# Layer 1, keys and values: the rows of all 25 tiles of nodes are summed, measured and normed ahead of the products

## The chip, the core and the metric

The program runs on one core of a Trainium2 chip. The metric is the device time of one launch in microseconds (us), as the median of three runs. Five engines work side by side and wait for each other through semaphores: TensorE (PE in the profile; PEld is its weight load), VectorE (DVE), ScalarE (ACT), GpSimd (POOL) and SyncE (SP, which only issues DMAs). DMAs are also issued from the queues of ScalarE and GpSimd.

## The reference, cut to what matters

Two layers of a graph network on 3125 nodes with 256 features (25 tiles of 128 nodes). Layer 0 ends with a mixture of experts with the two best experts of each node. Layer 1 begins with the sum of the experts' outputs, a layer norm, and from the normed rows both a sum over the graph's edges and a linear attention:

```python
x = x + _L0_ffn_ref(_layernorm(x)[None], ...)[0]      # gates[:, 0] * y0 + gates[:, 1] * y1
xn = _layernorm(x, axis=-1)
x = x + _L1_gnn_ref(xn, src, dst, edge_weight, ...) + _L1_mix_ref(xn[None], ...)[0]
# in _L1_gnn_ref
neighbor_emb = segment_sum(edge_val[:, None] * xn[edge_src], edge_dst)
# in _L1_mix_ref, _phi(x) = where(x > 0, x + 1, exp(x))
k_phi, v = _phi(xn @ Wk + bk), xn @ Wv + bv
kv, k_sum = einsum('blhd,blhe->bhde', k_phi, v), k_phi.sum(axis=1)
```

## The kernel before, in words

`build` runs the stages one after another, each a block at whose end all engines meet. The stage of this text is `keys_and_values`; ahead of it stands `gated_experts`, behind it `attend` (queries, attention and the output product) and `feed_forward`.

**What comes in.** The experts left two rows for each node in memory. They are loaded in five groups of five tiles (GT = 5), each group in two halves (s = 0 and 1, one for each of a node's two experts) of 640 KB, into three buffers `got`. Group g of g >= 3 takes the buffer of group g - 3 and waits for `taken` (line 1559).

**Rows.** For each tile VectorE adds the two halves with their gates into X (`add`, line 1601), measures the row (`measure`, line 1607, bn_stats), and for a part of several tiles works out the variance (`spreads`, lines 1615 to 1621). ScalarE takes the root (`roots`, line 1704), VectorE finishes 1/std and the shift (`scales`, lines 1628, 126 to 129 and 1630), and ScalarE writes the normed rows XN (`norm`, line 1708). SyncE stores each group of XN to `table` (line 1569). Before the change the three parts are tiles 0 to 4, 5 to 15 and 16 to 24. The first ten tiles are summed ahead of the products; the other fifteen are summed three at a time within steps 0 to 4, and tiles 5 to 24 are normed within steps 2 to 6.

**Steps.** There are 25 steps, one for each tile: TensorE turns the normed tile (line 1750), ScalarE copies it out (`keep`, line 1699), TensorE makes keys and values (line 1760), VectorE adds the bias (lines 1639, 1640) and cuts the negative part (line 1644), ScalarE takes its exponential (line 1734), VectorE puts the key together (line 1656), and TensorE adds it into the sum of key times value (line 1768).

**The head of the edges.** The nodes with most edges are treated by `Head`, one job a step for 24 steps. VectorE marks (`mark`, lines 825 and 836), ScalarE weighs with nine activations a job (`weigh`, line 846), TensorE multiplies (line 860) and every second step VectorE adds the result (line 884). ScalarE does jobs 0 and 1 directly behind `keep(0)`, and job i + 2 in step i. VectorE makes ready for them with eight short operations (`split_weights`, lines 784 to 787) and the marks of the first two jobs and of the first two groups of edges (lines 689, 697); before the change this stands ahead of the first sum.

**The other edges.** GpSimd waits until all five groups of `table` are stored and then gathers messages (`gather`, lines 654 and 656), six to a group of edges, for groups 0 to 5 at most: four groups of buffers, then one more group for each that TensorE has used (line 715). Groups 0 to 3 are used in steps 16, 19, 22 and 24. From group 6 on the gathers belong to the next block.

The order is written out by hand; each engine works off its own queue in the order of the code. On ScalarE, and this is what the change moves:

```python
roots(0); act.wait_ge(shift_ready, 1); norm(*parts[0])
load(act, 3, 1); load(act, 4, 1)
act.wait_ge(head.split, 8); keep(0)
for j in range(2): head.weigh(act, j)
for i in range(NT):
    if i + 1 < NT: keep(i + 1)
    if i in norming: norm(*norming[i])
    # exp of step i; weigh(i + 2); move of the edge groups beside step i
    if i in scaling: roots(scaling[i])
```

Of the kernel before, what the change touches and what calls it, by code (L numbers as in the profile page):

```python
# [19 lines left out]
NT = -(-N // P)  # L20
# [35 lines left out]
GT = 5  # L56
NG = NT // GT
# [1468 lines left out]
def keys_and_values(nc, const, routing, rows, cleared, X, XN, XNT, table, kv, kw, kv_bias, heads, more, edge_sums, groups, counts, digits, low, joint, room, counted):  # L1526
# [4 lines left out]
    parts = ((0, GT), (GT, 16), (16, NT))  # L1531
    adding = {i: range(2 * GT + 3 * i, 2 * GT + 3 * i + 3) for i in range(5)}
    scaling = {1: 1, 4: 2}
    norming = {2: (5, 9), 3: (9, 13), 4: (13, 16), 5: (16, 21), 6: (21, NT)}
    with ExitStack() as ctx:
# [30 lines left out]
        def _(sp):  # L1566
# [6 lines left out]
            for g in range(4):  # L1573
                load(sp, g, 0)
            store(0)
            load(sp, 4, 0)
            for g in range(1, NG):
                store(g)
# [13 lines left out]
        def _(dve):  # L1592
            c = Chain(dve, chain)
# [38 lines left out]
            def step(i):  # L1632
                k = i % 2
                more_rows = adding.get(i, ())
# [6 lines left out]
                for t in more_rows:  # L1641
                    add(t, 0)
                c.settle()
                ts(neg[k][:, :], key[k][:, :], 0.0, None, ALU.min).then_inc(cut, 1)
                for t in more_rows:
                    add(t, 1)
                if more_rows:
                    c.settle()
                for t in more_rows:
                    measure(t)  # L1650
# [10 lines left out]
                if i in scaling:  # L1661
                    spreads(scaling[i])
                    scales(scaling[i])
# [4 lines left out]
            head.split_weights(dve)  # L1668
            for j in range(2):
                head.mark(dve, j)  # L1670
            for e in range(2):
                edge_sums.mark(dve, e)
            for g in range(2):
                for i in range(g * GT, (g + 1) * GT):
                    add(i, 0)
                if g:
                    scales(0)
                c.settle()
                for i in range(g * GT, (g + 1) * GT):
                    add(i, 1)  # L1680
                c.settle()
                for i in range(g * GT, (g + 1) * GT):
                    measure(i)
                if g == 0:
                    spreads(0)
# [10 lines left out]
        def _(act):  # L1696
# [24 lines left out]
            load(act, 3, 1)  # L1721
            load(act, 4, 1)
# [4 lines left out]
            for i in range(NT):  # L1727
                if i + 1 < NT:
                    keep(i + 1)
                if i in norming:  # L1730
                    act.wait_ge(shift_ready, 2 if i < 5 else 3)
                    norm(*norming[i])
# [6 lines left out]
                if i in scaling:  # L1739
                    roots(scaling[i])  # L1740
# [1662 lines left out]
```

## Time and profile before

| | us |
|---|---|
| median of three runs (2177.54 to 2179.3) | 2177.92 |
| the profiled execution's own time | 2177.88 |
| its span (first to last instruction) | 2175.8 |
| TensorE busy in the span (83%) | 1802.7 |
| VectorE busy (57%) | 1249.2 |
| ScalarE busy (33%) | 708.5 |
| GpSimd busy (45%) | 984.2 |
| the stage `keys_and_values`, from 1134 to 1290 of the span | 156 |

Times in a row of the trace count from the start of the span. A row of the timeline has the start, how long the merged instructions took together, engine, line, operation, what is written and read, the count, and in brackets how long the engine had been idle and for whom. Instructions that overlap on one engine begin before the one ahead has ended, so that ten of 0.48 us take 4.16. The shares are means over stages with different limits; what this change is worth has to be read from its own stage.

### The profile page before, as it was taken

What the parts mean: (1) busy time and instruction counts of PE and PEld (TensorE: products, weight loads), DVE (VectorE), ACT (ScalarE), POOL (GpSimd) and SP (SyncE); (2) the same over time, 40 slices, a digit from 0 to 9 for tenths busy, and PEclk for the clock granted to TensorE, in tenths of its full rate; (3) what the DMA queues carried; (4) which work ended last, traced back from release to release, by engine and by line L of the source; (5) the groups of instructions that cost most, each with busy time, mean ns of one, the idle gap of its engine ahead of it and who ended that gap; (6) DMA issues with size and microseconds to landing.
All of it is one profiled execution on the core that took longest, in us unless ns stands there. A gap on an engine that the chain in (4) does not pass through costs nothing. (4 is left out here: it accounts for less than half of the span.)

```text
span 2175.8 us, 35585 instructions
## 1 busy us (share of the span) xinstructions
PE 1802.7 (83%) x10583; PEld 1413.6 (65%) x10584; DVE 1249.2 (57%) x3264; ACT 708.5 (33%) x1624; POOL 984.2 (45%) x1571
## 2 busy tenths in 40 slices
PE   7499689876485999999975999869999764999976
PEld 5266466554354999999962556546776642888865
DVE  6654796985565454444458657734454575333336
ACT  4222334443530121212127941123322231233324
POOL 0576786785111222222220547878877000455542
PEclk9999899988696999999986899979999886999998
DMA  7565554554641101011114324444444227122234
GB/s 237 153 155 139 151 143 122 148 139 109 252 182 46 37 29 37 30 36 33 33 48 138 97 61 158 114 124 112 137 123 122 86 90 320 56 65 63 65 80 133
DMA packets 171241, 239.50 MB, mean 110 GB/s; under 512 B 74145, under 2 KB 139261, under 8 KB 168692
## 3 DMA queue, kind: packets, MB, share of 16 engines
q0 software_dynamic: 42336, 112.74, 18.4%
q1 hardware_dynamic: 116884, 113.45, 16.1%
q10 hardware_dynamic: 11904, 11.96, 1.7%
q8 instruction: 47, 0.77, 0.1%
q14 instruction: 70, 0.57, 0.1%
HBM read 184.86 MB, written 56.12 MB: 111 GB/s over the span
## 5 line engine op out<-in xcount | busy, mean ns | idle before, releaser
L656 POOL DMA_INDIRECT agg_message<-table,edges_src x638 | 624.4, 979 | 177.7 <-POOL agg_rest L654 172.2
L2825 PEld LDWEIGHTS ex_p_h<-ex_xT,ex_own_up 128*128 128x128 f32 (+1 forms) x2464 | 281.3, 192 | 2.7 <-issue 1.4
L2825 PE MATMUL ex_p_h<-ex_xT,ex_own_up 128*128 128x128 f32 (+1 forms) x2464 | 282.0, 276 | 1.0 <-DVE ex_xT L2876 1.0
L2784 POOL DMA_INDIRECT ex_x<-moe_in,route_token_at x58 | 57.3, 987 | 311.8 <-PE ex_p_x L2815 242.3
L2880 DVE COPY ex_own_up<-moe_up 128x1280 f32 x114 | 100.5, 882 | 168.7 <-PE ex_p_h L2825 167.9
L654 POOL MEMSET agg_rest<- 128x1 f32 x638 | 75.6, 119 | 185.0 <-DMA table<-layer_XN 74.9
L715 PE MATMUL agg_partial<-agg_message,moe_up 128*64 128x321 f32 x638 | 113.7, 495 | 44.2 <-issue 22.0
L2950 POOL DMA_INDIRECT ex_x<-moe_in,route_token_at x66 | 64.3, 975 | 174.1 <-PE ex_p_x L2981 93.8
L2868 ACT ACTIVATE ex_gate_h<-ex_p_h 128x640 f32<-128x640 f32 x56 | 39.4, 704 | 315.3 <-PE ex_p_h L2825 315.3
L3021 ACT COPY ex_own_up<-moe_up 128x1024 f32 x66 | 68.9, 1046 | 209.9 <-PE ex_p_h L2994 169.4
L2994 PEld LDWEIGHTS ex_p_h<-ex_xT,ex_own_up 128*128 128x128 f32 x1024 | 119.3, 195 | 16.2 <-issue 14.9
L2994 PE MATMUL ex_p_h<-ex_xT,ex_own_up 128*128 128x128 f32 x1024 | 124.3, 281 | 4.7 <-issue 1.1
L3045 DVE TENSOR_SCALAR ex_hT<-ex_p_h,ex_up_b 128x128 f32<-128x128 f32 x256 | 72.1, 344 | 90.8 <-PE ex_p_h L2994 90.8
L3003 PE MATMUL ex_p_y<-moe_down,ex_hT 128*128 x512 | 115.8, 379 | 0.0
L727 ACT COPY agg_span<-agg_partial 128x321 f32<-128x321 f32 (+1 forms) x108 | 43.0, 398 | 216.4 <-PE agg_partial L719 201.2
L715 PEld LDWEIGHTS agg_partial<-agg_message,moe_up 128*64 128x64 f32 x638 | 47.6, 151 | 87.8 <-issue 60.0
L3003 PEld LDWEIGHTS ex_p_y<-moe_down,ex_hT 128*128 128x128 f32 x512 | 94.8, 190 | 11.5
L715 PE MATMUL agg_partial<-agg_message,agg_onehot 128*64 128x256 f32 x638 | 86.3, 407 | 19.1 <-PEq L111 8.7
L2793 POOL DMA_INDIRECT moe_out<-ex_y,route_row_at x56 | 56.6, 1012 | 81.8 <-DVE ex_y L2885 77.6
L2174 PE MATMUL ff_p_h<-ff_xT,layer_w 128*128 128x320 f32 x320 | 92.1, 441 | 0.5 <-ACT ff_xT L2105 0.5
L2189 PE MATMUL ff_p_y<-layer_w,ff_hT 128*128 128x256 f32 x400 | 90.2, 379 | 0.9 <-ACT ff_hT L2123 0.9
L719 PE MATMUL agg_partial<-agg_span,agg_shift 128*128 128x321 f32 (+2 forms) x212 | 85.6, 487 | 0.0
(666 smaller groups left out, 3708.3 us busy)
## 6 DMA issues: line engine op xcount, KB each, us to landing
moe_up<-in_f_w SPq DMA_DIRECT2D x8, 1386.0 KB, 20.1
agg_message<-in_edge_rows SPq DMA_DIRECT2D x54, 192.0 KB, 3.9
agg_message<-table,edges_src POOLq DMA_INDIRECT x638
sums<-agg_span SPq DMA_DIRECT2D x107, 80.2 KB
moe_up<-in_f_w SPq DMA_DIRECT2D x4, 2048.0 KB, 14.7
moe_down<-in_f_w SPq DMA_DIRECT2D x4, 2048.0 KB, 31.5
sums<-agg_span SPq DMA_DIRECT2D x107, 64.0 KB
moe0b_down<-in_f_w SPq DMA_DIRECT2D x8, 768.0 KB, 9.3
```

The costliest lines, as they stand in the source:

```text
L654: pool.memset(self.rest[:, :], 0.0).then_inc(self.paused, 1)
L656: pool.indirect_dma_start(out=to[:, k * w:k * w + D], out_offset=None, in_=self.table, in_offset=bass.IndirectOffsetOnAxis(ap=self.edges.s ...
L715: mm = pe.matmul(self.partial[h * W:(h + 1) * W, 0:w], hot[:, k * W:(k + 1) * W], msg[:, k * w:(k + 1) * w], start=(k % RUN == 0), stop=(g ...
L719: mm = pe.matmul(self.partial[to, 0:w], self.slot_shift(g)[:, to], self.held(g - 1), start=False, stop=True)
L2174: mm = pe.matmul(p_h[q % 2][:, s * 512:s * 512 + GH], w1_[:, c * FF + q * P:c * FF + (q + 1) * P], xT[:, c * GN + s * GH:c * GN + (s + 1) ...
L2189: mm = pe.matmul(p_y[n % 2][:, 0:D], hT[:, q * GN + n * P:q * GN + (n + 1) * P], w2_[:, q * D:(q + 1) * D], start=(q == 0), stop=(q == M - 1))
L2825: return pe.matmul(to, own_up[:, o:o + n], xT[:, k * D + c * P:k * D + (c + 1) * P], start=(c == 0), stop=(c == 1))
L2880: dve.tensor_copy(own_up[:, a:b], at(up, e * U0 + a, b - a)).then_inc(up_copied, 1)
L2994: mm = pe.matmul(p_h[k][:, q * P:(q + 1) * P], own_up[k][:, c * H1 + q * P:c * H1 + (q + 1) * P], xT[:, k * D + c * P:k * D + (c + 1) * P] ...
L3003: mm = pe.matmul(p_y[k][:, 0:D], hT[k][:, q * P:(q + 1) * P], at(down, ex[k] * (HQ * D) + q * D, D), start=(q == 0), stop=(q == HQ - 1))
L3021: act.copy(own_up[k][:, :], at(up, expert(act, r, k) * (2 * H1), 2 * H1)).then_inc(up_copied, 1)
L3045: ins = dve.tensor_scalar(hT[k][:, q * P:(q + 1) * P], p_h[k][:, q * P:(q + 1) * P], at(up_b, ex[k] * HQ + q, 1), 0.0, ALU.add, ALU.max)
```

## The change

All 25 tiles are summed and measured on VectorE ahead of step 0. The parts become tiles 0 to 4, 5 to 19 and 20 to 24; ScalarE takes the three roots and norms all 25 tiles before `keep(0)`. `split_weights` and the first marks move from ahead of the sums to behind them. SyncE issues the loads of groups 3 and 4 itself, both halves, in place of one half each on ScalarE, and all stores behind all loads.

```diff
-    parts = ((0, GT), (GT, 16), (16, NT))
-    adding = {i: range(2 * GT + 3 * i, 2 * GT + 3 * i + 3) for i in range(5)}
-    scaling = {1: 1, 4: 2}
-    norming = {2: (5, 9), 3: (9, 13), 4: (13, 16), 5: (16, 21), 6: (21, NT)}
+    parts = ((0, GT), (GT, 4 * GT), (4 * GT, NT))
+    measured = {0: 0, 3: 1, 4: 2}
...
-            for g in range(4):
+            for g in range(3):
                 load(sp, g, 0)
-            store(0)
-            load(sp, 4, 0)
-            for g in range(1, NG):
+            for g in range(3, NG):
+                for s in range(2):
+                    load(sp, g, s)
+            for g in range(NG):
                 store(g)
...
             def step(i):
...
-                for t in more_rows:
-                    add(t, 0)
...
-                for t in more_rows:
-                    add(t, 1)
-                if more_rows:
-                    c.settle()
-                for t in more_rows:
-                    measure(t)
...
-                if i in scaling:
-                    spreads(scaling[i])
-                    scales(scaling[i])
...
-            head.split_weights(dve)
-            for j in range(2):
-                head.mark(dve, j)
-            for e in range(2):
-                edge_sums.mark(dve, e)
-            for g in range(2):
+            for g in range(NG):
                 for i in range(g * GT, (g + 1) * GT):
                     add(i, 0)
-                if g:
-                    scales(0)
+                if g in (1, 4):
+                    scales(g // 4)
                 c.settle()
                 for i in range(g * GT, (g + 1) * GT):
                     add(i, 1)
                 c.settle()
                 for i in range(g * GT, (g + 1) * GT):
                     measure(i)
-                if g == 0:
-                    spreads(0)
+                if g in measured:
+                    spreads(measured[g])
+            scales(2)
+            head.split_weights(dve)
+            for j in range(2):
+                head.mark(dve, j)
+            for e in range(2):
+                edge_sums.mark(dve, e)
...
             norm(*parts[0])
-            load(act, 3, 1)
-            load(act, 4, 1)
+            for n in (1, 2):
+                roots(n)
+                act.wait_ge(shift_ready, n + 1)
+                norm(*parts[n])
             act.wait_ge(head.split, 8)
             keep(0)
...
-                if i in norming:
-                    act.wait_ge(shift_ready, 2 if i < 5 else 3)
-                    norm(*norming[i])
...
-                if i in scaling:
-                    roots(scaling[i])
```

What it does to the engines' queues, at the two places that the prediction speaks of. ScalarE, from the first root of the stage on, before (L1704 are roots, L1708 norms, L1699 `keep`, L846 `weigh`, L1734 the exponential):

```order
L1704 ACT_TABLE_LOAD
L1704 ACTIVATE kv_root<-kv_var 128x5
L1708 ACTIVATE layer_XN<-main_X,kv_shift,kv_rstd 128x256 x5
L1562 DMA kv_got<-moe_out 128x5x256 x2
L1699 COPY layer_XNT<-kv_p_x 128x2x128
L846 ACTIVATE layer_gw<-head_low,layer_gw 128x128 x9
L846 ACTIVATE head_pieces<-head_low,layer_gw 128x128 x9
L1699 COPY layer_XNT<-kv_p_x 128x2x128
L1734 ACT_TABLE_LOAD
```

The same place with the change, where these lines are L1692, L1696, L1687 and L1721:

```order
L1692 ACT_TABLE_LOAD
L1692 ACTIVATE kv_root<-kv_var 128x5
L1696 ACTIVATE layer_XN<-main_X,kv_shift,kv_rstd 128x256 x5
L1692 ACTIVATE kv_root<-kv_var 128x15
L1696 ACTIVATE layer_XN<-main_X,kv_shift,kv_rstd 128x256 x15
L1692 ACTIVATE kv_root<-kv_var 128x5
L1696 ACTIVATE layer_XN<-main_X,kv_shift,kv_rstd 128x256 x5
L1687 COPY layer_XNT<-kv_p_x 128x2x128
L846 ACTIVATE layer_gw<-head_low,layer_gw 128x128 x9
```

Twenty norms and two roots now stand ahead of `keep(0)`. With them go four table loads: before, each of the two later roots stood between exponentials and brought one for itself and one for the exponential behind it.

VectorE in step 0, from the bias on, before (L1601 are sums, L1607 measures):

```order
L1639 TENSOR_TENSOR kv_v<-kv_p_kv,kv_kb 128x2x128
L1640 TENSOR_TENSOR kv_key<-kv_p_kv,kv_kb 128x256
L1601 SCALAR_TENSOR_TENSOR main_X<-kv_got,main_gates,main_X 128x256 x3
L1644 TENSOR_SCALAR kv_neg<-kv_key 128x256
L1601 SCALAR_TENSOR_TENSOR main_X<-kv_got,main_gates,main_X 128x256 x3
L1607 BN_STATS kv_stats<-main_X 128x6 x3
L825 TENSOR_TENSOR head_low<-layer_w,edges_low 128x768
```

And with the change, from the two first jobs' marks on into step 0:

```order
L825 TENSOR_TENSOR head_low<-layer_w,edges_low 128x768
L836 TENSOR_SCALAR head_joint<-layer_w,edges_joint 128x100 x6
L689 TENSOR_SCALAR agg_onehot<-edges_node,edges_rel,edges_weight 128x64 x12
L697 TENSOR_SCALAR agg_shift<-edges_apart,edges_step 128x128
L1637 TENSOR_TENSOR kv_v<-kv_p_kv,kv_kb 128x2x128
L1638 TENSOR_TENSOR kv_key<-kv_p_kv,kv_kb 128x256
L1640 TENSOR_SCALAR kv_neg<-kv_key 128x256
L825 TENSOR_TENSOR head_low<-layer_w,edges_low 128x768
```

The sums and measures are gone from the steps; the first marks stand directly ahead of step 0, behind all sums.

## Rows read from the trace of the kernel before

**Rows 1.** Busy time by stretches of the stage; then clock, DMA share, GB/s

```profile
1134.00:1156.00 22.00, 1.24 (x4) 0.57 (x4) 20.00 (x70) 6.45 (x8) 3.02 (x2) 0.50 0.77 249
1156.00:1221.00 65.00, 46.79 (x187) 26.87 (x188) 45.03 (x154) 59.58 (x149) 6.43 (x12) 0.74 0.31 99
1221.00:1290.00 69.00, 66.35 (x332) 37.71 (x331) 45.47 (x147) 52.49 (x150) 33.20 (x62) 1.00 0.24 69
```

**Rows 2.** Timeline of ScalarE: keep(0), (1), (2), (10), (15)

```profile
1156.42 0.37 ACT L1699 COPY layer_XNT<-kv_p_x 128x256 f32<-128x256 f32 x1
...
1163.10 0.35 ACT L1699 COPY layer_XNT<-kv_p_x 128x256 f32<-128x256 f32 x1
...
1165.79 3.32 ACT L846 ACTIVATE layer_gw<-head_low,layer_gw 128x128 bf16<-128x128 bf16 x9 [0.61 <-DVE head_low L825]
1169.02 0.35 ACT L1699 COPY layer_XNT<-kv_p_x 128x256 f32<-128x256 f32 x1
...
1220.21 0.34 ACT L1699 COPY layer_XNT<-kv_p_x 128x256 f32<-128x256 f32 x1
...
1239.23 0.34 ACT L1699 COPY layer_XNT<-kv_p_x 128x256 f32<-128x256 f32 x1
```

**Rows 3.** Issues of ScalarE's first load of got, and its landing

```profile
L1562 ACTq DMA_DIRECT2D kv_got<-moe_out x1: 438/438/438, 1135.0 to 1135.0; - x1
DMA to landing us min/median/max: 6.9/6.9/6.9
```

**Rows 4.** Timeline of VectorE ahead of the steps

```profile
1136.05 1.50 DVE L786 CAST layer_gw<-edges_weight 128x72 bf16<-128x72 f32 x1
...
1138.35 0.20 DVE L786 CAST layer_gw<-layer_gw 128x72 bf16<-128x72 f32 x1
...
1139.55 0.56 DVE L825 TENSOR_TENSOR head_low<-layer_w,edges_low 128x768 bf16<-128x768 bf16 x1
...
1143.83 4.16 DVE L1601 SCALAR_TENSOR_TENSOR main_X<-kv_got,main_gates,main_X 128x256 f32<-128x256 f32 x10
...
1149.80 0.17 DVE L1615 TENSOR_TENSOR kv_mean<-kv_stats 128x5 f32<-128x5 f32 x1
...
1150.70 2.06 DVE L1601 SCALAR_TENSOR_TENSOR main_X<-kv_got,main_gates,main_X 128x256 f32<-128x256 f32 x5
1152.68 0.18 DVE L1628 RECIPROCAL kv_rstd<-kv_root 128x5 f32<-128x5 f32 x1
...
1153.70 0.17 DVE L1630 SCALAR_TENSOR_TENSOR kv_shift<-kv_mean,kv_rstd 128x5 f32<-128x5 f32 x1
...
1155.88 1.73 DVE L1607 BATCH_NORM_STATS2 kv_stats<-main_X 128x6 f32<-128x256 f32 x5
```

**Rows 5.** Timeline of ScalarE: a root and five norms

```profile
1197.80 0.21 ACT L1704 ACTIVATE kv_root<-kv_var 128x9 f32<-128x9 f32 x1
...
1199.32 2.57 ACT L1708 ACTIVATE layer_XN<-main_X,kv_shift,kv_rstd 128x256 f32<-128x256 f32 x5 [1.05 <-DVE kv_shift L1630]
```

**Rows 6.** Timeline of TensorE: steps 2 and 3

```profile
1169.42 3.78 PE L1760 MATMUL kv_p_kv<-layer_kw,layer_XNT 128*128 128x512 f32 x4 [1.84 <-ACT layer_XNT L1699]
1173.00 1.33 PE L860 MATMUL head_sum<-head_joint,layer_gw 128*128 128x150 bf16 x9
1174.12 1.16 PE L1768 MATMUL kv_p_a<-kv_v,kv_key 128*128 128x129 f32 x4
1175.07 0.63 PE L1750 MATMUL kv_p_x<-const_ident,layer_XN 128*128 128x128 f32 x2
1175.49 1.95 PE L1760 MATMUL kv_p_kv<-layer_kw,layer_XNT 128*128 128x512 f32 x4
```

**Rows 7.** Timeline of GpSimd: its first work, its first gather, the next block's first

```profile
1134.97 2.53 POOL L766 IOTA layer_w<- 128x768 bf16 x1 [3.24 <-POOLq L111]
...
1212.93 0.10 POOL L654 MEMSET agg_rest<- 128x1 f32 x1 [74.94 <-DMA table<-layer_XN]
...
1289.45 0.10 POOL L654 MEMSET agg_rest<- 128x1 f32 x1 [18.45 <-POOLq L111]
```

More of the change, by code:

```diff
@@ L1633, in step @@
                 k = i % 2
-                more_rows = adding.get(i, ())
                 dve.wait_ge(kv_made, i + 1)
```

## The prediction

> **What bounds the stage now.** The page's shares say nothing about one stage, so I cut the stage into stretches first [rows 1]. From 1134 to 1156 VectorE is the busy engine (20.0 of 22 us) and TensorE does next to nothing. From 1156 to 1221 it is ScalarE, 59.6 of 65 us; TensorE has 46.8 us and a granted clock of 0.74. From 1221 to 1290 TensorE has 66.4 of 69 us at full clock. So ScalarE sets the pace of the steps in the middle, and the question is what the change takes from it there and what it puts ahead of it.
>
> The timeline of ScalarE gives the pace [rows 2]. The start of `keep` (L1699) marks a step. From keep(10) at 1220.21 to keep(15) at 1239.23 there are five steps of 3.80 us: one copy, one exponential, nine weighings. From keep(0) at 1156.42 to keep(10) it takes 63.8 us, far more than ten times 3.80, because sums on VectorE, norms, roots and table loads on ScalarE and a half-clocked TensorE stand in those steps. That is what the change could win. The price is in front: keep(0) comes later. From keep(10) on both kernels do the same work in the same order, so the shift of keep(10) is the answer, if nothing behind it takes it up. I work out both halves.
>
> **First half: when keep(0) comes.** In the changed kernel VectorE has nothing ahead of the sums but three fills, so it waits for group 0. Its later half is issued at 1135.0 and lands 6.9 us after, at 1141.9 [rows 3]. The first sum starts then, not at 1143.83 [rows 4]: 1.9 us are won, though 7.8 us of work have been taken from in front of it, because that work was hiding the load.
>
> From there, with the distances in [rows 4]: a group of five tiles takes 1149.80 - 1143.83 = 5.97 us; `spreads` 1150.70 - 1149.80 = 0.90; group 1 with `scales(0)` in its midst runs from 1150.70 to the end of its measures at 1157.61, so 6.91. Groups 2 and 3 are two more of 5.97, then `spreads(1)` at 0.90. Group 4's first five sums and `scales(1)` are 1150.70 to 1153.87, so 3.17. Sum: 5.97 + 0.90 + 6.91 + 5.97 + 5.97 + 0.90 + 3.17 = 29.8, and the shift of part 1 is there at 1171.7.
>
> Do the loads keep up? The first stretch moved 249 GB/s on average with a DMA share of 0.77 [rows 1], so at a full share 249 / 0.77, about 320 GB/s (an estimate from this row). A group is 1.31 MB, 4.1 us, against 5.97 us of VectorE. Groups 3 and 4 are asked for when groups 0 and 1 are used and needed two groups later. I cost the loads at nothing; if one is late, its own 4.1 us is the price.
>
> ScalarE now norms 15 tiles: 3 x 2.57 = 7.7 us [rows 5], to 1179.4, and only behind them in its queue comes the root of part 2 (0.21), though VectorE has had the variance ready since 1171.7 + 2.06 + 1.73 + 0.90 = 1176.4. VectorE thus idles some 3.4 us. `scales(2)` takes 1153.87 - 1152.68 = 1.19 [rows 4], to 1181.1; the last five norms take 2.57, to **1183.7**.
>
> Behind `scales(2)` VectorE does `split_weights`, for which `keep(0)` waits too. Before, it took from 1136.05 to 1139.55, 3.50 us, but 1.30 of that is the first CAST (1.50, against 0.20 for the same cast later) while GpSimd filled its first iota from 1134.97 to 1137.50 [rows 4, 7]. GpSimd is long done with that at 1181, so I take 2.2 us and 1183.3, which leaves the norms as the last to come. The Trainium skill ("SBUF — State Buffer", section "SBUF: two separate sides") says that VectorE and GpSimd share a port pair under an exclusive lock; by that rule the long cast was a wait for the lock and won't recur. If it recurs after all, keep(0) is at 1184.6, 0.9 us later: this goes into the range. The marks (1139.55 to 1143.83, 4.28 us) end at 1187.6, before the first keys and values are made (below, keep(0) + 0.4 + 3.78 = 1187.9), so they lie beside TensorE.
>
> keep(0) comes at 1183.7, against 1156.42: **27.3 us later**.
>
> **Second half: from keep(0) to keep(10).** keep(1) comes after two jobs of weighing, 1163.10 - 1156.42 = 6.7 us, as before [rows 2]. keep(2): 1169.02 - 1163.10 = 5.9 less the 0.6 for which `weigh` waited for VectorE's mark behind the sums [rows 2], so 5.3 us (the table load for the exponential stays in it). Then eight steps of 3.80 = 30.4. Together 42.4 us, if TensorE keeps up.
>
> It doesn't quite. Step 2's products run at half clock now: 3.78 us for keys and values against 1.95 in step 3 [rows 6]. ScalarE's two jobs of weighing and the table load still leave TensorE with little before step 2, and I expect that again. At half clock TensorE needs 3.78 + 1.33 + 1.16 + 0.63 = 6.9 us for step 2 [rows 6]; started 0.35 us behind keep(2), at keep(0) + 12.35, it is through at + 19.3, step 3's product (1.95, full clock) at + 21.2, and VectorE's bias and cut (1.1 us) let ScalarE go on at + 22.3. On ScalarE's own pace that exponential stood at + 19.9. So 2.4 us are lost once; from then on TensorE has less than 3.80 us of work a step. Total 42.4 + 2.4 = **44.8 us, 19.0 less than the 63.8 before**. Which half clock stretches stay is the weak point. The Trainium skill ("TensorE: Matmul & The Clock Gate", section "HAM oscillation") says that bursts with waits between them let the clock fall again; by that rule the short bursts of steps 0 to 2 are throttled here too, and the dense steps behind are not.
>
> **Behind keep(10): nothing.** The table is complete earlier: the last norm ends at 1183.7 instead of about 1209, so gathers start some 25 us sooner than 1212.93. They end in four groups of buffers and wait for TensorE's step 16. In the third stretch TensorE is busy 66.4 of 69 us and so waits for no message [rows 1]; GpSimd instead stood 18.45 us at the end until the next block began [rows 7]. Early gathers have no taker. SyncE's stores and the four small loads behind them also move forward, with no one waiting. Four table loads of ScalarE are gone; they are part of the 19.0, not added to it.
>
> **Sum.** + 27.3 - 19.0 = + 8.3 us. 2177.88 + 8.3 = 2186.2. The profiled execution is at the median of the runs (2177.92), so the forecast for the median is **2186.2 us**. Sums between the products were nearly free only where another engine was last; still, 15 tiles ahead cost 27 us with the norms and the idle root, and took 19 from the steps.
>
> **Rivals.**
> 1. *TensorE has its full clock from step 2 on.* For it: the steps are denser. Against: steps 0 to 2 contain the same waits for ScalarE. The 2.4 us go: + 5.9, 2183.8.
> 2. *Half clock lasts longer.* If two further steps run at half clock, each takes 7.1 us of TensorE (6.9 and a little for wider jobs) instead of 3.80 of ScalarE: + 3.3 each, so + 14.9, 2192.8. For it: the second stretch had a mean clock of 0.74 [rows 1], so that half clock (0.50) held for about half of it. Against: it lay behind waits for sums and norms that are gone.
> 3. *The stored table is what the end waits for* (the other side). If groups 0 to 5 or what follows them hung on the gathers, the stage's end would come forward with them. It decides if any product of edges waits for its messages. All 25 us would turn + 8.3 into - 17, so 2161; a third of it would just cancel the loss. Against: the 18.45 us that GpSimd stood idle, and a TensorE without gaps in the last stretch [rows 1, 7]. This needs the trace to hide a wait.
> 4. *The loads are late.* One group late by its own 4.1 us: + 12.4, 2190.3. Against: the estimate of 4.1 against 5.97 us.
>
> Even if every step ran at ScalarE's 3.80 from keep(0) on, keep(0) to keep(10) would be 38.0 us, and the change still + 1.5 us. That is the lower end of what the steps can give, and it excludes a gain by this path.
>
> **How the numbers follow.** Forecast 0.60; rival 1 0.14; rival 2 0.08; rival 4 0.07; rival 3 0.05; and 0.06 that something unpriced (steps at the lower end, or a later stage that takes up the shift) brings it to between 0 and + 4. A measurement of this kernel tells 0.2%, 4.4 us, from no change. Slower by more than that: forecast and rivals 1, 2 and 4, less 0.03 for rival 1 with a keep(0) that is 1.5 us early: 0.86. Within: 0.06 + 0.03 = 0.09. Faster: 0.05. The forecast's own terms: keep(0) by - 1 (marks and loads better) to + 1 (the long cast), the clock by - 2.4 to + 3.3 (one step more at half clock). The range reaches down past rival 1 to + 3.1 and up to rival 4: 2181 to 2191.
>
> **What the profile would show.** Right: VectorE's first sum at about 1142; a gap of 3 to 4 us on VectorE before the last `scales`; keep(0) at 1184 (1 us either way); keep(10) at 1228.5; keep-to-keep 3.80 us from step 4 on; one table load for the exponential in the stage; first gather near 1187, with a GpSimd idle ahead of step 16 and again at the block's end; the next block's start some 8 us later than 1289.5, and everything behind it shifted by the same. Wrong: sums that wait for a landing between groups (rival 4), a half clock in steps 4 to 6 (rival 2), TensorE waiting for messages in the kernel before and not now (rival 3), or the next block's start shifted by 8 us but the end of the program not.

## The result, and the profile after

| | before | after |
|---|---|---|
| median of eight runs, same chip (us) | 2178.09 | 2186.11 |
| ratio, 95% interval | | 1.0034 [1.0023, 1.0044] |
| the same two kernels in the next comparison | 2178.99 | 2184.06 |
| ratio | | 1.0023 [1.0014, 1.0032] |
| span of the profiled execution | 2175.8 | 2184.4 |

The changed kernel is slower, by 8.0 us in the first comparison and 5.1 us in the second. The forecast was 2186.2, + 8.3 us. The profile says that this agreement is better than the reasons behind it.

I cut the trace in pieces whose ends both kernels have: *ahead* (to VectorE's first fill of the stage), *keys and values* (to `attend`'s first product on TensorE), *attend* (to GpSimd's first row in `feed_forward`), and the *rest*. For the two kernels and their repetitions:

| us | ahead | keys and values | attend | rest |
|---|---|---|---|---|
| before | 1135.3 | 154.2 | 143.1 | 743.2 |
| before, again | 1137.8 | 154.2 | 143.2 | 743.1 |
| after | 1137.2 | 159.6 | 145.2 | 742.5 |
| after, again | 1133.9 | 159.2 | 146.2 | 744.1 |

*Ahead* is the same code in all four and scatters by 4 us; the rest scatters by 1.6. The stage itself is sharp: 154.2 against 159.2 to 159.6, so **5.0 to 5.4 us** are lost in it. And `attend`, which the change does not touch, is **2 to 3 us** longer in both profiles of the changed kernel. Whether that comes from the change is a question of its own, and the runs below leave it open.

**The stage.** The heads of the page of after; before, TensorE was busy for 1802.7 us and ScalarE for 708.5, in 1624 instructions. The four table loads are gone.

```profile
span 2184.4 us, 35581 instructions
PE 1794.8 (82%) x10583; PEld 1409.7 (65%) x10584; DVE 1247.7 (57%) x3264; ACT 703.2 (32%) x1620; POOL 986.5 (45%) x1571
```

The stretches of [rows 1] in the kernel after (columns as there):

```profile
1134.00:1156.00 22.00, 1.24 (x4) 0.57 (x4) 12.53 (x42) 6.38 (x8) 3.02 (x2) 0.50 0.85 274
1156.00:1221.00 65.00, 31.82 (x150) 18.88 (x151) 47.68 (x167) 46.78 (x125) 25.52 (x48) 0.68 0.40 126
1221.00:1290.00 69.00, 68.61 (x344) 39.30 (x344) 45.53 (x144) 59.07 (x169) 13.53 (x25) 1.00 0.12 33
```

In the middle stretch ScalarE has 46.8 us of work instead of 59.6 and TensorE 31.8 instead of 46.8: work has moved out of it, because ScalarE and TensorE now start their steps later. VectorE's timeline, which answers to [rows 4], says how late:

```profile
1143.88 4.17 DVE L1600 SCALAR_TENSOR_TENSOR main_X<-kv_got,main_gates,main_X 128x256 f32<-128x256 f32 x10 [5.85 <-DMA kv_got<-moe_out]
...
1181.27 0.19 DVE L1627 RECIPROCAL kv_rstd<-kv_root 128x5 f32<-128x5 f32 x1 [2.86 <-ACT kv_root L1692]
...
1182.38 0.19 DVE L786 CAST layer_gw<-edges_weight 128x72 bf16<-128x72 f32 x1
...
1184.30 0.56 DVE L825 TENSOR_TENSOR head_low<-layer_w,edges_low 128x768 bf16<-128x768 bf16 x1
```

The first sum waits 5.85 us for the load and starts 6.7 us behind the stage's first fill (1137.20); the forecast had 6.6. No group behind it waits for a landing. The last `scales` waits 2.86 us for a root that stands behind 15 norms in ScalarE's queue. `split_weights` takes 1182.38 to 1184.30, 1.9 us: its first cast is 0.19 us, not 1.50 as in [rows 4]. The same on ScalarE, which answers to [rows 2]:

```profile
1150.89 0.21 ACT L1692 ACTIVATE kv_root<-kv_var 128x5 f32<-128x5 f32 x1 [9.00 <-DVE kv_var L1620]
...
1173.67 7.47 ACT L1696 ACTIVATE layer_XN<-main_X,kv_shift,kv_rstd 128x256 f32<-128x256 f32 x15 [2.96 <-DVE kv_shift L1629]
1181.05 0.19 ACT L1692 ACTIVATE kv_root<-kv_var 128x5 f32<-128x5 f32 x1
1182.50 2.57 ACT L1696 ACTIVATE layer_XN<-main_X,kv_shift,kv_rstd 128x256 f32<-128x256 f32 x5 [1.26 <-DVE kv_shift L1629]
1184.97 0.35 ACT L1687 COPY layer_XNT<-kv_p_x 128x256 f32<-128x256 f32 x1
...
1191.64 0.35 ACT L1687 COPY layer_XNT<-kv_p_x 128x256 f32<-128x256 f32 x1
1192.01 1.28 ACT L1721 ACT_TABLE_LOAD   x1
...
1196.84 0.35 ACT L1687 COPY layer_XNT<-kv_p_x 128x256 f32<-128x256 f32 x1
...
1227.48 0.34 ACT L1687 COPY layer_XNT<-kv_p_x 128x256 f32<-128x256 f32 x1
```

keep(0) comes at 1184.97, 47.8 us behind the first fill; before it was 1156.42 - 1135.30 = 21.1. So it is 26.7 us later. keep(0) to keep(10) takes 1227.48 - 1184.97 = 42.5 us against 63.8, so 21.3 shorter. The difference is + 5.4, the whole loss of the stage. TensorE's half clock did come (its timeline, which answers to [rows 6]), but it ended before step 2. Steps 0, 1 and 2 in the kernel after:

```profile
1185.37 3.78 PE L1745 MATMUL kv_p_kv<-layer_kw,layer_XNT 128*128 128x512 f32 x4 [29.51 <-ACT layer_XNT L1687]
...
1192.05 3.78 PE L1745 MATMUL kv_p_kv<-layer_kw,layer_XNT 128*128 128x512 f32 x4 [1.70 <-ACT layer_XNT L1687]
...
1197.79 2.01 PE L1745 MATMUL kv_p_kv<-layer_kw,layer_XNT 128*128 128x512 f32 x4
```

The four products of steps 0 and 1 took 3.78 us each time and those of step 2 took 2.01. The granted clock was 0.50 until 1198 and 0.99 to 1.00 from there to keep(10). Before, step 1 had full clock already, but the clock fell again while the steps waited: steps 2 [rows 6], 4, 6 and 7 took 3.78 us.

```profile
1163.51 1.98 PE L1760 MATMUL kv_p_kv<-layer_kw,layer_XNT 128*128 128x512 f32 x4 [1.68 <-ACT layer_XNT L1699]
```

These falls are gone. Step 1 now lies beside ScalarE's table load and nine weighings (keep(1) to keep(2), 5.2 us), so its half clock cost next to nothing: the pace was ScalarE's own, 42.4 us by the forecast's count and 42.5 measured. In the repeated run step 1's products took 2.60 us and keep(0) to keep(10) 42.3.

**Attend.** GpSimd gathers through the whole of it, some 1.33 us a gather, and stops only where a buffer is not free. Its timeline in the kernel after: first gather of the stage, the wait for step 16, attend's first, the wait for a product of attend, `feed_forward`'s first:

```profile
1188.95 0.10 POOL L654 MEMSET agg_rest<- 128x1 f32 x1 [49.05 <-DMA table<-layer_XN]
...
1255.80 0.10 POOL L654 MEMSET agg_rest<- 128x1 f32 x1 [34.28 <-PE agg_partial L715]
...
1296.74 0.10 POOL L654 MEMSET agg_rest<- 128x1 f32 x1 [18.45 <-POOLq L111]
...
1325.46 0.10 POOL L654 MEMSET agg_rest<- 128x1 f32 x1 [3.55 <-PE agg_partial L719]
...
1441.94 0.10 POOL L654 MEMSET agg_rest<- 128x1 f32 x1 [0.47 <-POOLq L111]
```

and the kernel before, where attend's first is in [rows 7]:

```profile
1316.48 0.10 POOL L654 MEMSET agg_rest<- 128x1 f32 x1 [2.22 <-PE agg_partial L719]
...
1432.59 0.10 POOL L654 MEMSET agg_rest<- 128x1 f32 x1 [0.47 <-POOLq L111]
```

The stage's gathers behave as forecast: 24 us earlier in the span (25.9 counted from the stage's first fill), then 34.3 us of idle for step 16, and 18.45 us at the block's end as before. In attend, GpSimd waits for the product of edge group 5, whose buffer it needs after 18 gathers. Before, that wait ends 27.0 us behind attend's first gather; after, 28.7; in the repeated run 30.0. From there to the end it is 116.1, 116.5 and 116.2. So 1.7 of the 2.1 us, and 2.9 of the 3.1, arise before that product. TensorE's first row in attend, before, after, and after again:

```profile
1289.49 4.54 PE L1930 MATMUL att_p_q<-layer_XNT,layer_qw 128*128 128x320 f32 x16 [1.74 <-PEq L111]
```

```profile
1296.78 6.24 PE L1915 MATMUL att_p_q<-layer_XNT,layer_qw 128*128 128x320 f32 x16 [1.74 <-PEq L111]
```

```profile
1293.12 7.49 PE L1915 MATMUL att_p_q<-layer_XNT,layer_qw 128*128 128x320 f32 x16 [1.74 <-PEq L111]
...
1323.06 0.10 POOL L654 MEMSET agg_rest<- 128x1 f32 x1 [4.88 <-PE agg_partial L719]
```

The same 16 products take 4.54, 6.24 and 7.49 us, and GpSimd's wait is 2.22, 3.55 and 4.88. The granted clock over attend's first 10 us (in these rows the number behind the busy times) is 1.00, 0.83 and 0.70:

```profile
1289.50:1299.50 10.00, 10.00 (x47) 7.32 (x48) 7.58 (x26) 1.53 (x2) 7.80 (x15) 1.00 0.28 80
1296.80:1306.80 10.00, 10.00 (x39) 6.72 (x40) 5.89 (x21) 1.53 (x2) 7.53 (x16) 0.83 0.27 80
1293.10:1303.10 10.00, 9.98 (x33) 6.42 (x34) 5.24 (x20) 0.68 (x1) 7.53 (x16) 0.70 0.27 80
```

Taken by single microseconds, the clock is at half for about 3 us in after (from 1297 on) and for about 6.5 in the repeated run (from 1292.4 on). The product that GpSimd waits for starts later by just what the 16 products took longer. Before, after, and after again:

```profile
1314.28 1.51 PE L715 MATMUL agg_partial<-agg_message,agg_onehot 128*64 128x256 f32 x12
```

```profile
1323.25 1.52 PE L715 MATMUL agg_partial<-agg_message,agg_onehot 128*64 128x256 f32 x12
```

```profile
1320.85 1.51 PE L715 MATMUL agg_partial<-agg_message,agg_onehot 128*64 128x256 f32 x12
```

Counted from attend's first product these are 24.8, 26.5 and 27.7 us: 1.7 and 2.9 later, and the 16 products took 1.7 and 2.95 longer. So the loss is in the main a piece of half clock around the block's end, and GpSimd carries it on: its wait makes up 1.3 and 2.7 us of attend's 2.1 and 3.1. The other 0.4 to 0.7 us lie in the gathers themselves; what made those longer is not shown.

### The profile page after: what moved, and what is told of

Same layout as the page of the kernel before. It is cut to its first block and busy times, and to the rows that moved or that the text cites. A ratio compares the mean times of both kernels' runs of the same rounds, so it can differ in the third digit from the quotient of the medians.

```text
span 2184.4 us, 35581 instructions
## 1 busy us (share of the span) xinstructions
PE 1794.8 (82%) x10583; PEld 1409.7 (65%) x10584; DVE 1247.7 (57%) x3264; ACT 703.2 (32%) x1620; POOL 986.5 (45%) x1571
```

## The experiments

Twelve runs, two of them the same two kernels again, in three comparisons on three chips. My theory of the stage: its 5.4 us come from norms and a root ahead of keep(0) while the weighing stands behind it. Its rivals: the clock in the steps makes the loss, or the moved marks make it. Of attend I first expected scatter between executions (theory A of the first two runs); from filled_end on the theory was TensorE's clock at attend's start. The expectations count attend to `feed_forward`'s first large product on TensorE, some 14.5 us behind the end used here, so that their 157.6 is 143.1 in the table; and they count keep(0) to its end, 0.35 us behind its start. The table has the lengths of the pieces, and the medians against the kernel before in the same comparison (2178.99, 2178.80, 2179.26).

| us | keys and values | attend | median | ratio, 95% interval |
|---|---|---|---|---|
| b_again | 154.2 | 143.2 | 2179.14 | 0.9997 [0.9988, 1.0006] |
| a_again | 159.2 | 146.2 | 2184.06 | 1.0023 [1.0014, 1.0032] |
| weigh_early | 154.6 | 143.3 | 2178.32 | 0.9995 [0.9986, 1.0004] |
| tables_back | 166.4 | 144.8 | 2192.88 (four runs) | 1.0057 [1.0042, 1.0073] |
| filled_end | 160.0 | 143.3 | 2184.79 | 1.0028 [1.0019, 1.0038] |
| root_early | 158.1 | 144.8 | 2183.94 | 1.0020 [1.0011, 1.0029] |
| joined | 154.0 | 144.6 | 2179.12 | 0.9998 [0.9989, 1.0007] |
| jobs_ahead | 153.6 | 143.3 | 2178.11 | 0.9992 [0.9983, 1.0001] |
| marks_ahead | 161.2 | 143.1 | one run, 2186.11 | |
| before_sooner | 154.2 | 140.1 | 2176.02 | 0.9984 [0.9975, 0.9993] |
| after_sooner | 159.3 | 140.2 | 2179.53 | 1.0004 [0.9995, 1.0013] |
| jobs_sooner | 153.7 | 140.2 | 2176.15 | 0.9984 [0.9975, 0.9993] |

**The two kernels again** (no edit).

> The kernel before, unchanged, for a second profile. Theory A (only the stage keys_and_values differs between the kernels, the 1.9 us ahead of it and the 2.0 us in attend are scatter between executions): from the stage's first VectorE work to attend's first product 154.2 us as in the first profile, within 0.5 us; attend, from its first product to feed_forward's first, anywhere from 157.5 to 160 us; the start of the stage anywhere from 1134 to 1138. Theory B (the shift in attend belongs to the change): attend 157.6 us again, within 0.3 us.

> The changed kernel again, with a second profile. Theory A: the stage 159.6 us again, 5.4 longer than before, and against the kernel before a ratio of about 1.0025 (5.4 us). Theory B (attend is really 2 us longer too): attend 159.7 us again and a ratio of about 1.0035 (7.5 us).

The stage's two lengths come back within 0.4 us. Attend is 143.2 and 146.2: that of the kernel before came back within 0.1 us and that of the kernel after was long again, which speaks against the scatter that theory A expected (after_sooner, below, brings it back in part). The kernel after is + 5.1 us here, + 8.0 in the first comparison; a median moves by up to 2 us from one comparison to the next, and *ahead* by more between the profiles.

**weigh_early: ScalarE weighs while it waits for sums.**

```diff
+            head.split_weights(dve)
+            for j in range(2):
+                head.mark(dve, j)
+            for e in range(2):
+                edge_sums.mark(dve, e)
             for g in range(NG):
...
-            head.split_weights(dve)
-            for j in range(2):
-                head.mark(dve, j)
-            for e in range(2):
-                edge_sums.mark(dve, e)
...
+            act.wait_ge(head.split, 8)
+            keep(0)
+            for j in range(2):
+                head.weigh(act, j)
             for n in (1, 2):
                 roots(n)
                 act.wait_ge(shift_ready, n + 1)
                 norm(*parts[n])
-            act.wait_ge(head.split, 8)
-            keep(0)
-            for j in range(2):
-                head.weigh(act, j)
```

> The changed kernel, with the split of the weights and the first marks back ahead of the sums, and keep(0) and the weighing of jobs 0 and 1 put on ScalarE behind the first five norms, where it is idle while VectorE sums. Theory A (keep(0) to keep(1), 6.7 us, stands on the path only because it is queued behind the norms): the first sum comes 1.9 us later, keep(1) follows the last norm at once; keep(10) 4.8 us earlier than in the changed kernel counted from the stage's start, or 2.4 us less of a gain if step 2 falls to half clock: 2180 to 2184 us where the changed kernel has 2186. Rival (TensorE, idle until then, sets the first steps): no gain over the changed kernel, 2186.

ScalarE in weigh_early:

```profile
1155.83 0.35 ACT L1687 COPY layer_XNT<-kv_p_x 128x256 f32<-128x256 f32 x1
1156.09 3.31 ACT L846 ACTIVATE layer_gw<-head_low,layer_gw 128x128 bf16<-128x128 bf16 x9
1159.30 3.31 ACT L846 ACTIVATE head_pieces<-head_low,layer_gw 128x128 bf16<-128x128 bf16 x9
1169.89 0.21 ACT L1692 ACTIVATE kv_root<-kv_var 128x15 f32<-128x15 f32 x1 [7.28 <-DVE kv_var L1620]
...
1184.37 0.35 ACT L1687 COPY layer_XNT<-kv_p_x 128x256 f32<-128x256 f32 x1
```

The 6.7 us of weighing lie in what was a 14 us idle for sums; keep(1) comes 49.6 us behind the first fill (1134.77), where after has it at 54.4. The stage is 4.6 to 5.0 us shorter than in the two profiles of after, attend starts at full clock (4.55 us), and the kernel is level with before. At 2178.32 us it came out below the expected 2180 to 2184, and 5.7 us below a_again: the stage and, by the profile, attend's full clock. The loss of the stage is work that ScalarE does in the open while it had idled earlier. This part of the theory holds.

**marks_ahead: only VectorE's marks back** (the first part of the edit above, to tell it from the weighing).

> The changed kernel with the split of the weights and the first marks back ahead of the sums, nothing else. Theory A (ahead of the sums they lie beside the load of the first group, so that only 1.9 of their 7.8 us delay the first sum, and behind the sums they lie beside ScalarE's norms and TensorE's first product): keep(0) 1.9 us later in the stage, 50.0 us in place of 48.1, the stage 161.3 us; moving them behind was right by 1.9 us. Rival (half their time is on the path behind the sums): no difference or a gain.

keep(0) comes 1.8 us later and the stage is 1.6 to 1.9 us longer than after's: taken alone, the marks ahead of the sums cost something, since they now delay the first sum past the landing (8.5 us behind the first fill instead of 6.7). What weigh_early gained is therefore not theirs. Attend started at full clock here (4.54 us) and took 143.1, though the whole lead of the change stands in front of it.

**root_early: the last root in the midst of the norms.**

```diff
-            for n in (1, 2):
-                roots(n)
-                act.wait_ge(shift_ready, n + 1)
-                norm(*parts[n])
+            roots(1)
+            act.wait_ge(shift_ready, 2)
+            norm(GT, 3 * GT)
+            roots(2)
+            norm(3 * GT, 4 * GT)
+            act.wait_ge(shift_ready, 3)
+            norm(*parts[2])
```

> The changed kernel with the root of tiles 20 to 24 put between the norms of tiles 14 and 15, so that VectorE no longer waits 2.9 us for it and ScalarE not 1.3 us for VectorE. Theory A (the chain up to keep(0) is VectorE's sums, 15 norms, root, scales, five norms): keep(0) 1.3 us earlier in the stage, at 46.8 us in place of 48.1, everything behind it as before, the stage 158 us. Attend is 157.7 us or 159.7 and more, as the clock falls at the stage's end or not; with theory B of the first runs (attend is longer because of what the change moved) it stays at 159.7 or more. Rival (VectorE's split of the weights and marks bind instead): keep(0) moves by under 0.5 us.

ScalarE in root_early:

```profile
1176.92 5.00 ACT L1696 ACTIVATE layer_XN<-main_X,kv_shift,kv_rstd 128x256 f32<-128x256 f32 x10
1181.83 0.35 ACT L1687 COPY layer_XNT<-kv_p_x 128x256 f32<-128x256 f32 x1
```

Ten norms run without the 1.26 us wait of after. keep(0) is 46.3 us behind the first fill instead of 47.8, and the stage 1.2 to 1.5 us shorter. Timed, this is within what a median moves.

**tables_back: two pairs of table loads put back into the steps.** The added root's result is not used.

```diff
+                if i in (1, 4):
+                    act.activation(again[:, 0:GT], var[:, 0:GT], ACT.Sqrt)
```

> The changed kernel with one root more on ScalarE behind steps 1 and 4 (its result is used by nothing), so that the four table loads that the change removed are back, with no sums or norms in the steps. Theory A (ScalarE sets the pace of steps 0 to 10, so that whatever is put on it there is on the path): keep(0) to keep(10) 42.5 + 4 x 1.28 + 0.4 = 48.0 us, and the whole 5.5 us longer than the changed kernel. Rival (TensorE's clock takes it up): the waits bring half clock back and it is 8 us or more. Rival (slack): under 2 us.

ScalarE in tables_back; L1728 is the added root:

```profile
1200.53 1.28 ACT L1728 ACT_TABLE_LOAD   x1
1201.83 0.21 ACT L1728 ACTIVATE kv_again<-kv_var 128x5 f32<-128x5 f32 x1
1201.94 0.35 ACT L1688 COPY layer_XNT<-kv_p_x 128x256 f32<-128x256 f32 x1
1202.31 1.28 ACT L1722 ACT_TABLE_LOAD   x1
1203.60 0.42 ACT L1722 ACTIVATE kv_neg<-kv_neg 128x256 f32<-128x256 f32 x1
...
1212.15 0.42 ACT L1722 ACTIVATE kv_neg<-kv_neg 128x256 f32<-128x256 f32 x1 [0.89 <-DVE kv_neg L1641]
```

A load takes 1.28 us and the next activation begins 1.30 us after it began. keep(2) at 1196.47 to keep(4) at 1207.13 is 10.7 us here and 1204.67 - 1196.84 = 7.8 in after, so a pair with its root adds 2.8 us, and both some 5.7 us. The stage grew by 6.8 to 7.2; the rest goes with a piece of half clock at which ScalarE waited 0.89 us for VectorE, which waited for TensorE (granted clock 0.50 from 1207.9 to 1211.3). So what the change removed there was worth about 5.7 us, the two small roots included, and the 21.3 us gained in the steps contain it. The Trainium skill ("ScalarE: Activation LUTs", section "What ACT_TABLE_LOAD costs") adds a drain of about 1.38 us to each load, 2.66 in all; an estimate by that page's figure is 10.6 us for the four. The rows here do not agree: they show no second part.

**filled_end: TensorE gets products at the stage's end,** so that it does not idle before the block's end. They write a buffer that nobody reads any more.

```diff
+            def fill(n):
+                pe.wait_ge(kept, NT)
+                for k in range(n):
+                    pe.matmul(p_x[0][:, 0:D], const.ident[:, :], XN[:, 0:D], start=True, stop=True)
...
+            fill(2)
             into_kv(NT - 1)
+            fill(3)
```

> The changed kernel with five products that nothing reads added on TensorE at the stage's end (two ahead of the last into_kv, where it waits 0.9 us for VectorE, three behind it, where it waits for the other engines to meet), so that TensorE is not idle there. Theory A (the 2 to 2.8 us that attend lost come from the granted clock, which fell to half as TensorE stood idle at the stage's end, and attend's first products then ran at half clock): full clock at attend's first product, attend 157.7 us in place of 159.7 and 160.5, the stage 159.2 to 160.0 us; 2 us less than the changed kernel. Rival (attend lost the time by something else, the moved stores or gathers): attend stays at 159.5 us or more.

Attend's first products, then GpSimd's wait in attend:

```profile
1293.92 4.54 PE L1922 MATMUL att_p_q<-layer_XNT,layer_qw 128*128 128x320 f32 x16 [1.25 <-PEq L111]
...
1320.92 0.10 POOL L654 MEMSET agg_rest<- 128x1 f32 x1 [2.26 <-PE agg_partial L719]
```

With the fill, attend starts at full clock (4.54 us), the wait is 2.26 as in the kernel before, and attend takes 143.3. That fits the link of clock, wait and length. It does not show that the fill kept the clock up: it is one profile, and marks_ahead and, below, after_sooner start attend at full clock without any fill. Counted to the expectation's end attend took 159.0 us here, not 157.7: the first products of `feed_forward` came some 1.2 us later behind the end used in the table, which I did not follow. The fill itself makes the stage 0.5 to 0.8 us longer (from keep(24) to attend's first product 12.3 us instead of 11.5), and the timed median did not fall: + 6.0 us against before, where after has + 5.1 and + 8.0. The expected 2 us were seen in the profile, not in the time.

**joined: weigh_early, root_early and filled_end in one.**

> weigh_early (marks and the first two jobs of weighing ahead), root_early and filled_end together. Theory A: the stage 154.6 - 1.3 + 0 to 0.5 = 153.3 to 153.8 us, attend 157.7, so 1 us under the kernel before. Rival (TensorE's half clock at steps 1 and 2 takes the 1.3 us up): the stage 154.6 again.

The stage is 154.0, only 0.6 less than weigh_early's. The early root did its part: keep(24) comes 141.7 us behind the first fill instead of 143.0, so 1.4 us earlier, and the fill took 0.8 of it back (12.3 us from keep(24) to attend, as in filled_end). Attend has a second wait of 1.74 us at its next group, where before has 0.75; I did not follow it. The median is level with before, not 1 us below it as expected.

**jobs_ahead: four jobs ahead instead of two,** joined with the steps' jobs shifted by two on VectorE and TensorE and the weighings by four in all. The marks of the two further jobs then stand between VectorE's sums (not in the cut).

```diff
-            for j in range(2):
+            for j in range(4):
                 head.weigh(act, j)
...
-                    head.weigh(act, i + 2)
+                    head.weigh(act, i + 4)
...
-                head.on_vector(dve, i)
+                head.on_vector(dve, i + 2)
...
-                head.on_tensor(pe, i)
+                head.on_tensor(pe, i + 2)
```

> joined, with four jobs of the edges' head weighed on ScalarE and two multiplied on TensorE while VectorE sums, in place of two and none; each step then does the job two further on. Theory A (ScalarE's weighings set the pace of the steps, and those at 3.3 us each that stand beside the sums cost nothing): two weighings (6.6 us) go from the steps, less 1.7 us of marks that VectorE does between sums and less what TensorE, nearly full from step 14 on, gives back: the stage 3 to 5 us shorter than joined, 149 to 151 us, the whole 2173 to 2175 where the kernel before has 2179. Rival (from step 10 on TensorE is the bound, busy 66.4 of 69 us): under 1.5 us.

Stretches of the stage in jobs_ahead, and ScalarE in one of its last steps:

```profile
1188.00:1240.00 52.00, 49.41 (x249) 29.84 (x250) 32.81 (x104) 51.97 (x149) 26.03 (x48) 0.97 0.30 89
1240.00:1290.00 50.00, 49.49 (x245) 27.81 (x243) 31.76 (x102) 30.85 (x87) 12.74 (x24) 1.00 0.16 43
```

```profile
1274.43 0.42 ACT L1726 ACTIVATE kv_neg<-kv_neg 128x256 f32<-128x256 f32 x1 [2.46 <-DVE kv_neg L1640]
```

Two more weighings left the steps, and the stage lost 0.4 us against joined, where 3 to 5 were expected. Two things stand against the gain. keep(1) comes at 50.8 us instead of 48.2, so 2.5 later, with the further marks and their wait between the sums; behind it the stage is 2.9 us shorter, less than half of the 6.6 that left. And TensorE is busy 98.9 of 102 us from 1188 to 1290, while ScalarE drops to 30.9 of the last 50 and waits up to 2.46 us a step for VectorE, which waits for TensorE. In these steps moving work on ScalarE or VectorE has little left to gain; no run here tests it further.

**The other half: attend's wait.** Three kernels with the product of edge group 5 brought forward, directly behind the first products of attend; in before, in after, and in jobs_ahead.

```diff
-        ahead, beside = groups[:1], spread(groups[1:], NT)
+        ahead, second, beside = groups[:1], groups[1], spread(groups[2:], NT)
...
-            for e in ahead:
+            for e in (*ahead, second):
                 edge_sums.mark(dve, e + 2)
...
+            edge_sums.move(act, second)
...
             mm.then_inc(head_made, 1)
+            edge_sums.products(pe, second)
             pe.wait_ge(headed, 1)
```

> The kernel before, with attend's second group of edges (group 5) multiplied directly behind the head's 25 products instead of in the second turn of the loop, so that its buffer comes free some 7 us sooner. Theory A (attend is as long as GpSimd's gathers plus its waits for buffers, 2.22 and 0.8 us in the kernel before): both waits gone, GpSimd's 18 groups of attend done 140.2 us behind attend's first product in place of 143.1, and the whole 2 to 3 us shorter. Rival (TensorE binds in attend, GpSimd's waits cost nothing): the waits go and attend stays at 143 us.

> The changed kernel with the same edit. Theory A (the 2 to 3 us that attend lost with the change are GpSimd's wait for that one product, 3.6 to 4.9 us in place of 2.2, because TensorE's first products in attend ran at half clock): with the product sooner the half clock costs nothing, attend 140.2 us as in the line above, whether the clock falls or not; the whole 5.3 us over before_sooner, 3 us over the kernel before. Rival (attend is longer for another reason): 2 to 3 us longer than before_sooner's attend.

> jobs_ahead with the same edit. Theory A: the stage 153.6 us and attend 140.2, so 3.5 us under the kernel before: 2175.3 where it has 2178.8. Rival: attend 143 us, 0.7 us under it.

GpSimd in before_sooner: attend's first gather and `feed_forward`'s first. No wait for a product stands between them.

```profile
1292.46 0.10 POOL L654 MEMSET agg_rest<- 128x1 f32 x1 [18.45 <-POOLq L111]
...
1432.64 0.10 POOL L654 MEMSET agg_rest<- 128x1 f32 x1 [0.47 <-POOLq L111]
```

Attend takes 140.14, 140.18 and 140.19 us in the three: 3.0 less than in before, 5.0 to 6.0 less than in after. The 3.0 are before's two waits in attend, 2.22 and 0.75 us: attend is as long as GpSimd's gathers and its waits. What the three do not show is that a half clock costs nothing once the product is sooner. All three began attend at full clock (4.54 us), so this half of after_sooner's expectation was not put to the test. Two of the three are faster than the kernel before, by 3.2 and 3.1 us: 2176.02 and 2176.15, ratio 0.9984 [0.9975, 0.9993]. after_sooner is level with it, where 3 us over it were expected. Against before_sooner it is + 5.1 us in the stage by the profiles (159.3 - 154.2) and + 3.5 timed.

## Why the prediction was right, and where only its sum was

- **keep(0)** (+ 27.3 forecast): measured + 26.7. First sum, no late load (rival 4 fell), the idle of VectorE for the late root (3.4 forecast, 2.86 measured) and the short cast all came as worked out. Of the 0.6 us too many, 0.3 are the 15 norms, which took 7.4 us rather than 7.7, and 0.3 are a slip in the sum: 1179.4 with a root of 0.21 and `scales` of 1.19 gives 1180.8, not 1181.1, and an idle of 3.2 us, not 3.4.
- **keep(0) to keep(10)** (44.8 forecast): measured 42.5. The term that failed is "*At half clock TensorE needs 6.9 us for step 2 ... So 2.4 us are lost once*". ScalarE's part of the sum, 42.4, was right to 0.1; the half clock covered steps 0 and 1, where ScalarE had more to do than TensorE, and was over at step 2 (2.01 us for its products instead of 3.78). The half clock of step 2 in [rows 6] was a second fall, behind a step 1 at full clock; the prediction carried it over, and it did not come again. So it is rival 1 that came true, TensorE at full clock from step 2 on (+ 5.9; measured + 5.4). The end of the half clock scatters: step 1's products took 3.78, 2.60 and 2.75 us in the three profiles with this same stage (after, a_again, after_sooner), and step 2's 1.98 to 2.01. In tables_back it came back in step 4, behind the added loads, and once more around 1219.
- **"Behind keep(10): nothing"** was wrong. Inside the stage it held: early gathers had no taker, and rival 3 fell, since GpSimd just waited 34.3 us at step 16. But I had looked for a taker of the shift only up to the stage's end. The next block's chain ran through GpSimd and had a wait of 2.22 us on a product of TensorE in the trace of before; a slower start of TensorE there went on into the end: + 2 to 3 us in the two profiles. That the change itself slows this start is not shown (see below).
- **The sum.** The stage was forecast at + 8.3 and came out at 26.7 - 21.3 = 5.4, so 2.9 us were too many there, and 2 to 3 us were missing in attend. The two errors cancelled, so the hit on + 8.3 is luck. It is luck in the measuring too: the first comparison gave + 8.0 us, the second + 5.1, and 1.9 of the 8.6 us between the two profiled executions lie in *ahead*. The medians alone would have hidden that; the pieces of the profile did not.
- **The bound** "+ 1.5, no gain by this path" held for this change; weigh_early shows what it rested on, keep(0) behind all norms with the weighing behind keep(0). With the weighing in the idle, the same 25 tiles ahead cost 0.4 us in the stage and nothing in the time.

What stays open. Attend began at a reduced clock in four of the six profiles that keep the change's long lead without early weighing or fill (after, a_again, root_early, tables_back; not marks_ahead and after_sooner) and in none of the others (before, b_again, before_sooner, weigh_early and the four with a fill). TensorE's idle at the block's end is 1.74 us in all without a fill. root_early and tables_back repeat the link: 6.24 us for the 16 products and a wait of 3.55, as in after. Why the same idle costs the clock in some and not in others I did not settle. The stage of after_sooner is after's to the letter and ended at full clock, so the fall comes and goes between executions of the same code; that the change makes it more likely is a count, not a proof. Nor is it settled why *ahead*, the same code, takes 1133.6 to 1138.3 us, a scatter as large as the loss of the stage.

## What to carry to other kernels

Work that is moved ahead of a pipeline costs the first step's delay less what it took from the pace of the steps: work out both, by the engine that sets the pace, and then fill the idle that the move opens on that engine (here two weighings, 5 us). Ask what bounds the *next* block too: if its chain waits for an engine that your block leaves in another state, a stage that is sharp to 0.4 us can still move the end. And look at waits of 2 us on a chain that runs for 140: against the kernel before, bringing one product forward was worth 3 us, and all that was tried on the stage itself at most 0.6.

## What the runs showed of the hardware

- A table load on ScalarE took 1.28 us, the next activation began 1.29 to 1.30 us after its start, and four with two roots cost 5.7 us where ScalarE set the pace (tables_back).
- The first cast of `split_weights` took 1.50 us beside GpSimd's iota and 0.19 us without it, in every profile of either order that was read for it (1.50 in before, b_again, weigh_early and marks_ahead, 0.19 in after, a_again and after_sooner).
- The same 16 products took 4.54, 6.24 or 7.49 us at a block's start, with the same 1.74 us of idle ahead of them. Another engine, GpSimd, paid for it (2.22, 3.55, 4.88 us of wait).
- With one and the same stage in front (after, a_again, after_sooner) these products took 6.24, 7.49 and 4.54 us: the clock at a block's start is not fixed by the code.
